# A fused decoder layer: queries and attention output in PSUM banks of their own, the scores of key tile 1 in the bank of tile 3

## What is computed

```
x = x + layernorm(attention(layernorm(x)))
x = x + layernorm(moe(layernorm(x)))

attention: q = rope(x @ Wq.T)                    16 heads of 128
           kp, vp = x @ Wkv.T                     one key and one value row per position
           k[h] = rope(kp * kh[h]); v[h] = vp * vh[h]     kh, vh: gated running sums
           p = softmax(causal(q k / sqrt(128)))
           o = p v;  return o @ Wout.T
moe:       8 experts of width 176, the best 2 per position, capacity 640 rows each,
           and a shared expert of width 704
```

## Time and profile before

| what | value |
|---|---|
| runs shown | 798.91, 798.91, 800.09 us; median 798.91 |
| profiled execution | 800.48 us, of which the span of the profile is 798.5 us |
| busy share of the span | PE 93%, PEld 78%, DVE 72%, ACT 59%, POOL 68% |
| chain that ended last, by engine | PE 73%, DVE 11%, issue 7%, ACT 4%, POOL 2%, DMA 2% |
| chain that ended last, most costly lines | L432 21%, L968 16%, L933 13%, L984 9%, L954 7%, all PE |
| L968, all in the loop | 512 matmuls, 149.5 us busy, mean 434 ns |
| L1340, all in the loop | 64 products, 44.3 us busy, mean 692 ns |

### The profile page before, as it was taken

How to read it: one execution, slowest core, us unless ns; L and a number is a source line. 1 busy time by engine, 2 the same in 40 slices (tenths; PEclk the granted TensorE clock), 3 DMA queues, 4 the chain that set the end, 5 groups by cost and what they waited for, 6 DMA issues and landing times.

```text
span 798.5 us, 14037 instructions
## 1 busy us (share of the span) xinstructions
PE 745.3 (93%) x4364; PEld 625.8 (78%) x4364; DVE 574.3 (72%) x1536; ACT 467.6 (59%) x1163; POOL 543.1 (68%) x459
## 2 busy tenths in 40 slices
PE   5799999999999999999999999998999989899992
PEld 4577788888888888887777888777778878898761
DVE  6967886768777767778887777898572357775685
ACT  5557776766676767666567666565623255653432
POOL 4457998787878887778888988778533534433663
PEclk9999999999999999999999999999999999999997
DMA  9411346422122222221222222221151134532332
GB/s 299 126 46 53 91 159 184 147 68 68 67 67 68 67 68 67 68 64 57 69 74 73 87 73 56 65 74 48 54 159 41 64 142 174 183 144 86 110 98 90
DMA packets 47748, 75.73 MB, mean 95 GB/s; under 512 B 9728, under 2 KB 24640, under 8 KB 47680
## 3 DMA queue, kind: packets, MB, share of 16 engines
q1 hardware_dynamic: 43504, 65.19, 25.9%
q0 software_dynamic: 3072, 8.39, 3.3%
q10 hardware_dynamic: 1104, 1.31, 0.5%
HBM read 57.71 MB, written 17.17 MB: 94 GB/s over the span
## 4 chain that ended last, share of the span: by engine, by line
PE 73%; DVE 11%; issue 7%; ACT 4%; POOL 2%; DMA 2%; DVEq 0%; ACTq 0%; POOLq 0%
PE ps L432 21%; PE ps L968 16%; PE ps L933 13%; PE ps L984 9%; PE ps L954 7%; PE ps L1130 5%; DVE q_sw L1312 1%; DVE q_sw L1311 1%; DVE hid_both L1643 1%; POOL slot_inputs L1784 1%; DVE hid_hi L1633 1%; POOL o_lo L1768 1%; DVE hid L1638 1%; DVE hid L1630 1%; DMA kvh_rows<-hc_t 1%
## 5 line engine op out<-in xcount | busy, mean ns | idle before, releaser
L968 PE MATMUL ps<-pt,vp 128*128 128x512 f32 (+3 forms) x512 | 149.5, 434 | 10.3 <-DVE q_sw L1312 10.1
L633 ACT ACTIVATE prob<-ps,neg_max 128x512 f32<-128x512 f32 (+3 forms) x256 | 132.5, 525 | 33.4 <-DVE neg_max L1321 30.6
L968 PEld LDWEIGHTS ps<-pt,vp 128*128 128x128 f32 x512 | 82.7, 190 | 59.9 <-issue 30.5
L1749 POOL TENSOR_TENSOR q_sw<-q_cos,q_sw 128x512 f32<-128x512 f32 x62 | 79.2, 1277 | 65.9 <-DVE q_cos L1313 65.8
L1321 DVE CUSTOM_DVE_ANT_0 ps<-ps,causal_row 128x512 f32<-128x512 f32 (+3 forms) x256 | 120.2, 511 | 4.6 <-PE ps L933 4.5
L642 ACT ACTIVATE pt<-ps,vcol 128x512 f32<-128x512 f32 x64 | 44.2, 690 | 109.4 <-PE ps L954 109.4
L1768 POOL TENSOR_TENSOR o_lo<-o_t,o_hi 128x512 fp32r<-128x512 f32 x64 | 84.4, 1318 | 33.4 <-ACT o_hi L671 33.4
L954 PE MATMUL ps<-id_f,prob 128*128 128x128 f32 x640 | 92.3, 275 | 0.9 <-ACT pt L642 0.9
L933 PE MATMUL ps<-k_hi,q_hi 128*128 128x512 f32 x248 | 86.6, 349 | 0.4 <-POOL q_lo L1753 0.3
L1340 DVE TENSOR_TENSOR o_t<-ps,inv_row 128x512 f32<-128x512 f32 x64 | 44.3, 692 | 52.5 <-PE ps L968 52.5
L1753 POOL TENSOR_TENSOR q_lo<-q_sw,q_hi 128x512 fp32r<-128x512 f32 x62 | 80.2, 1294 | 2.6 <-ACT q_hi L665 2.3
(11 more groups left out here) (218 smaller groups left out, 1942.3 us busy)
## 6 DMA issues: line engine op xcount, KB each, us to landing
kh_row<-kvh_rows SPq DMA_DIRECT2D x64, 256.0 KB, 3.2
inv_row<-inverse_sums SPq DMA_DIRECT2D x64, 256.0 KB, 3.1
slot_inputs<-zeros SPq DMA_DIRECT2D x8, 640.0 KB, 4.9
xg<-slot_inputs SPq DMA_DIRECT2D x8, 640.0 KB, 4.5
slot_outputs<-yo SPq DMA_DIRECT2D x8, 640.0 KB, 3.3
up_raw<-in_w_up_dram SPq DMA_DIRECT2D x8, 368.0 KB, 4.5
wo_raw<-in_wout_dram SPq DMA_DIRECT2D x4, 512.0 KB, 7.9
dn_sb<-in_w_dn_dram SPq DMA_DIRECT2D x8, 256.0 KB, 3.5
```

The lines of the kernel that those rows point to most:

```text
L633: ins = act.activation(prob[:, i % 2, ROW_AT[nt]:ROW_AT[nt] + w], ps_s[bank][:, at:at + w], ACT.Exp, scale=-1.0, bias=neg_max[:, i % 2, nt ...
L968: ins = pe.matmul(ps_qo[:, mt * P:SEQ], vp[:, b * TPB + mt, :], pt[:, i % 2, cols], start=(mt == 0), stop=(mt == PT_BANKS[-1][-1]))
L1749: pool.tensor_tensor(q_sw[:], q_cos[:], q_sw[:], ALU.add).then_inc(q_sum_ready, 1)
```

## The change

- Bank 0 holds queries alone (`ps_q`), bank 3 the attention output alone (`ps_o`). For units from 2 on the scores of tile 1 go to columns 0 to 255 of bank 1, behind those of tile 3: they wait until the exponentials of tile 3 of the same unit have read it, and the scores of tile 3 of a unit wait for all the exponentials of the unit before.
- `queries` waits for the rope products of the unit before only, `weigh_values` no longer for rope products.
- The routing pieces keep columns 256 and up of bank 3, now beside the output: `weigh_values(i)` waits until the former piece is out (`bank_free`, formerly `spare_free`), a piece waits for the divide of its step. `route_piece(i)` moves to the end of the step.
- The third group of scores moves behind `weigh_values`; the maxima and the exponentials of it move behind the divide and behind the output head.
- On VectorE `inverses(i + 1)` moves behind the layer norm and routing work of its step.

The diff without the renamed uses of the buffers and indices:

```diff
 PT_BANKS = [[0], [1, 3], [2]]
 
 
-def s_slot(nt):
-
-    return {3: (0, 0), 2: (1, 0), 0: (1, 384), 1: (2, 0)}[nt]
+def s_slot(i, nt):
+
+    return {3: (0, 0), 2: (1, 0), 0: (1, 384), 1: (0, 0) if i >= 2 else (2, 0)}[nt]
 
 
 def pt_slot(mt):
...
             return ctx.enter_context(nc.semaphore(name))
 
         ps = [ctx.enter_context(nc.psum_tensor(f"ps{i}", [P, 512], F32)) for i in range(8)]
-        ps_qo = ps[0]
+        ps_q = ps[0]
+        ps_o = ps[3]
         ps_s = [ps[1], ps[2], ps[3]]
         ps_pt = [ps[4], ps[5]]
         ps_acc = [ps[6], ps[7]]
...
                 if i == FACTOR_STEP:
                     factors_as_columns(1)
                 if i + 2 < UNITS:
-                    exps(i + 2, [1, 2])
+                    exps(i + 2, [1])
                 if i == UNITS - 2:
                     x_normed(ROUTED)
                 head_of_output(i)
+                if i + 2 < UNITS:
+                    exps(i + 2, [2])
                 for b, n in routes(i):
                     if 0 <= n < 4:
                         head_of_quarter(b, n)
...
                 if i:
                     pe.wait_ge(q_sin_ready, i)
                     pe.wait_ge(q_cos_ready, i)
-                if i >= 4:
-                    pe.wait_ge(o_ready, i - 3)
                 if i < H:
                     pe.wait_ge(wq_ready, wq_part(i) + 1)
                 h, b = head(i), batch(i)
-                three_pass(pe, ps_qo[:], lambda o: wq_hi[:, h, o, :], lambda o: wq_lo[:, h, o, :],
+                three_pass(pe, ps_q[:], lambda o: wq_hi[:, h, o, :], lambda o: wq_lo[:, h, o, :],
                            lambda o: xt_hi[:, o, tok(b)], lambda o: xt_lo[:, o, tok(b)]).then_inc(q_psum, 1)
 
             def scores(i, groups=range(3)):
...
                 r = i % 2
                 for k in groups:
                     tiles = S_BANKS[k]
-                    if i:
+                    if i >= 2 and k == 2:
+                        pe.wait_ge(exp_ready, 3 * i + 1)
+                    elif i >= 3 and k == 0:
+                        pe.wait_ge(exp_ready, 3 * i)
+                    elif i:
                         pe.wait_ge(exp_ready, 3 * (i - 1) + (k + 1))
                     for nt in tiles:
-                        bank, at = s_slot(nt)
+                        bank, at = s_slot(i, nt)
                         w = P * (nt + 1)
                         qs = slice(nt * P, (nt + 1) * P)
                         passes = ((q_rot, kh),) if i < PLAIN else ((q_hi, k_hi), (q_hi, k_lo), (q_lo, k_hi))
...
                     ins.then_inc(pt_psum, 1)
 
             def weigh_values(i):
-                n = min(i + 4, UNITS)
-                pe.wait_ge(q_sin_ready, n)
-                pe.wait_ge(q_cos_ready, n)
                 if i:
                     pe.wait_ge(o_ready, i)
+                else:
+                    pe.wait_ge(exp_ready, 6)
+                bank_free(i)
                 b = batch(i)
                 for k, tiles in enumerate(PT_BANKS):
                     pe.wait_ge((pt_first_ready, pt_second_ready, pt_rest_ready)[k], i + 1)
                     for mt in tiles:
                         cols = slice(COL_AT[mt], COL_AT[mt] + SEQ - mt * P)
-                        ins = pe.matmul(ps_qo[:, mt * P:SEQ], vp[:, b * TPB + mt, :], pt[:, i % 2, cols],
+                        ins = pe.matmul(ps_o[:, mt * P:SEQ], vp[:, b * TPB + mt, :], pt[:, i % 2, cols],
                                         start=(mt == 0), stop=(mt == PT_BANKS[-1][-1]))
                 ins.then_inc(o_psum, 1)
 
...
                         pe.wait_ge(pos_taken, b + 1)
 
             def route_piece(i):
-                spare_free(i)
                 for b, n in routes(i):
-                    if 0 <= n < 10 and i + 2 < UNITS:
-                        pe.wait_ge(exp_ready, 3 * (i + 2))
+                    if 0 <= n < 10:
+                        pe.wait_ge(o_ready, i + 1)
                     if 0 <= n < 4:
                         turn_quarter(b, n)
                     elif 4 <= n < 6:
...
                 if i + 2 < UNITS:
                     scores(i + 2, [0, 1])
                 turn_probs(i, [2])
-                route_piece(i)
-                if i + 2 < UNITS:
-                    scores(i + 2, [2])
                 if i == UNITS - 1:
                     turn(ROUTED)
                 weigh_values(i)
+                if i + 2 < UNITS:
+                    scores(i + 2, [2])
                 if i == FACTOR_STEP:
                     turn_factors(1)
                 if i == 1:
...
                     gather_output(i - 1)
                 if i + 4 < UNITS:
                     queries(i + 4)
+                route_piece(i)
             gather_output(UNITS - 1)
 
             def shared_up(j, tiles=range(SH)):
...
                     scaled_gates(1)
                 if i == 5:
                     sums_of_gates(1)
-                if i + 1 < UNITS:
-                    inverses(i + 1)
                 for b in range(B - 1):
                     n = i - back_step(b)
                     if n == 0:
...
                         choose(b)
                     elif n == POSITIONS + 1:
                         find_slots(b)
+                if i + 1 < UNITS:
+                    inverses(i + 1)
                 if i > 1 and wo_head(i - 2) is not None:
                     rest_of_wo(wo_head(i - 2))
                 if i + 3 < UNITS:
...
                     maxima(i + 2, [0])
                 rest_turned(i)
                 if i + 2 < UNITS:
-                    maxima(i + 2, [1, 2])
+                    maxima(i + 2, [1])
                 if i == UNITS - 1:
                     rest_of_turned(ROUTED)
                 divide_output(i)
+                if i + 2 < UNITS:
+                    maxima(i + 2, [2])
                 if i == 0:
                     dve.wait_ge(kt_ready, B)
                 if i == UNITS - 3:
```

## The result

The changed kernel takes 813.96 us (median of 6 runs, 812.52 to 816.39), the kernel before beside it 800.1 us (6 runs, 798.91 to 800.97): a ratio of 1.018, with an interval of 1.0159 to 1.0201. It is slower by 13.9 us where 7.7 were predicted, and 0.5 us above the range's top. The profiled execution is the slowest of the six, 816.39 us with a span of 814.4. That is 15.9 us over the span before. Among the six the span falls to 810.5 us as the mean granted clock of TensorE rises from 0.979 to 0.987 (0.989 in the profile before).

What follows compares the result with a forecast made beforehand. The prediction took TensorE alone to bound a plain step, with VectorE's lateness deciding its stalls. Terms -0.1 + 3.8 + 2.4 + 1.6 - 0.6 + 0.6 = +7.7 on 798.91 gave 806.6 us, range 798.0 to 813.5.

Steps and rivals of the forecast that it cites:

- The loss of 0.48 a quarter: Steps with a quarter routing piece: VectorE's rope products delayed 1.25 us, losing 0.48 each; eight steps, +3.8 us.
- 1.20 for the best experts: Two best-experts steps, waiting for turned logits: delay 1.97 us, loss 1.20 each, +2.4 us in all.
- 0.77 us as the time to spare: How late VectorE may be after the change before `weigh_values` loses time waiting for `rest_turned`; 0.48 us before.
- variances and shifts: Four stalls at 4-column VectorE operations held by GpSimd's run: `inverses` now uncovered, 0.44 - 0.29 each, +0.6 us.
- The start: First steps: queries stop waiting for the divide, tile-1 scores wait for late tile-3 exponentials (+2.5); together -0.1 us.
- step 3's stall: A stall of 1.36 us, predicted to be swallowed by the +2.5 us wait for exponentials in step 2.
- the 1.22 of the sum: First step: queries of unit 4 no longer wait for the divide, -0.98 - 0.24 = -1.22 us.
- The choice: Two steps choosing experts: same work, looser wait, -0.3 us each, -0.6 us in all.
- Slots: Two steps waiting for positions: delay 3.07 us, loss 2.30 against 1.49 before, +1.6 us in all.
- A: Rival, faster: the rope-product wait simply goes in nine late steps; 785.4 us at best, some 793 with pieces; chance 0.13.
- B: Rival, no change: routing pieces are absorbed with 1.25 us to spare instead of 0.77; 798.1 us; chance 0.11.
- C: Rival, much slower: no delay absorbed because the tile-1 chain binds the next step too; 812 to 819.7 us; chance 0.11.

Runs made afterwards that it cites:

- the run with the transposes: Changed kernel plus 19 unused identity transposes on TensorE in step 2, during its wait for the tile-3 exponentials: 813.0 us, ratio 1.0155.
- the repaired one: Changed kernel with `inverses` first on VectorE, routing pieces ahead of the queries, sigmoids later in step 2 and scatter DMAs moved: 794.8 us, ratio 0.9936.
- split changed kernel: The repaired one with `choose` and `find_slots` each cut into two halves in two steps: 801.83 us, ratio 1.0023.
- the run with the waits kept: Changed kernel with the two waits of `weigh_values` for the rope products of unit i + 3 kept: 830.74 us, ratio 1.0392.

## Why the prediction was half right

**The mechanism held.** `weigh_values` waits for `rest_turned`, the former wait for the divide at 64.35 is gone, TensorE waits for the tile-3 exponentials near 80 us, the chain holds `inverses` behind the routing work, and quarter steps take 8.7 us where "about 8.6" stood. The loss of 0.48 a quarter measured 0.53 to 0.61, that of 1.20 for the best experts 1.01 and 1.09. So 0.77 us as the time to spare was right within 0.2.

**The term that failed most: variances and shifts, +0.6, measured +5.0.** The step was "0.44 - 0.29, four times", from "`inverses` ran before it, covered; now behind, uncovered". Two things are missing. The blocked operation lasts until GpSimd's run ends, and that run ends later in the step. By the timelines of both kernels the run itself is 7.74 us long in both (394.10 to 401.84, and 400.86 to 408.60), and the operation lasts 4.61 us for 3.46 only because VectorE comes to it earlier. But the run ends 2.94 us behind the first transposes of the step (405.66) instead of 2.23 (399.61), and `inverses` stands behind it. With `inverses` back ahead these steps still take 9.91 and 9.73 us, 0.34 above before. There VectorE waits 1.04 us ahead of `inverses` in the step before, for tile 1's exponentials, which the change moved back (0.18 us in the kernel before); that this is the 0.34 was not tried apart. Second, the stall grew from 1.37 us to 2.08 and 1.88, and TensorE's clock fell behind it. The prediction has no term for that. By the start-to-start times from the weighing's two matmuls to the queries (3.87 and 3.70 us, 2.59 in a quarter step), 1.3 and 1.1 us of the +5.0 are half clock, plus 0.2 in the queries of batch 1. In the run with the transposes, where a stall of the same 2.08 us left the clock at 1.00, step 41 and the step behind take 10.43 + 7.98 us instead of 11.09 + 8.75, so 1.4 less. The rest of the +5.0, some 2.4, is the longer delay.

**The start, -0.1, measured +2.1.** The waits came as costed: 2.38 us of idle time for "+2.5", and step 3's stall was swallowed. The wait at the first queries is gone too; from the first scores to the first gather TensorE takes 10.86 us instead of 11.91, so 1.05 for the 1.22 of the sum. What was not in the sum is the half clock behind it, 1.5 us by the run with the transposes. The longest idle time of TensorE in the loop of before was 1.37 us, and the text took a wait of 2.5 us for no more than 2.5 us.

**The choice, -0.6, measured +1.2.** It was called "same work, looser wait". But the step ahead is late. With the best experts the rope products start 2.09 us behind the first transposes (363.24 against 361.15) instead of 0.25 (357.32 against 357.07), and GpSimd's products, which follow them, now run beside VectorE's next work: a layer norm operation (at 368.09) and the first of the choice, of 4 columns, take 1.26 and 1.25 us instead of 0.37 and 0.16, while a later one of 32 columns, 1.20 us before, takes 0.23. With pieces ahead of the queries 0.3 to 0.4 us of a choice step goes, with `inverses` ahead 0.13 to 0.15.

**Slots, +1.6, measured +0.5.** The sign was right, the size a third. GpSimd is idle from 388.84 and the two operations took 0.54 us, so the rope products came 2.74 us late (at 390.68, with the step's first transposes at 387.90, less the usual 0.04) and not the 3.07 assumed. The loss is 1.76 us a step (9.85 less 7.96 and the 0.13 of the positions), 0.27 above the 1.49 of before, where the sum had 2.30. The Trainium skill, GPSIMD Engine Reference, section Key points, says that GpSimd and VectorE instructions with two SBUF inputs contend. The trace agrees: the two operations take 1.40 us beside a busy GpSimd, 0.54 where it stops on the way, and 0.29 beside an idle one (the third batch, at 593.11 in the kernel before).

**The rivals.** A fell: the wait did not simply go. B fell: quarter steps were not 8.2 us. C named the total (812 to 819.7) but not the cause, for tile 1's chain ends nothing last in the loop beyond step 2. The half clock is in no case of the prediction. In the profiled execution it is 1.5 + 1.3 + 1.3 = 4.1 us; with it taken off, the +15.3 would be +11.2 against +7.7.

The Trainium skill, Perfetto Trace Analysis, section Matmuls, has independent groups rotate through banks, so that the emptying of one overlaps the next group. The trace agrees where the bank is what is waited for (16.8 us in the new order). Private banks give nothing that can be told where the next wait in the queue stands close behind (794.8 against 793.32 us): at choice and slots the kernel before with moved scatters waits 0.87 and 1.25 us for rope products, the repaired one 0.83 and 0.83 us for `rest_turned`.

## What to carry to other kernels

Ahead of taking a resource conflict away, list what stands behind it in the waiting engine's queue: the next wait in the same queue may be 0.29 us away, and the order that comes with the new freedom may cost more than it gives (813.96 against 800.1 us here). When work moves on one engine, look at what then waits for it on the others: with the scores moved on TensorE alone, the divide stood behind a maximum that came later. Move work on an in-order engine only after having looked at what covered it: `inverses` cost nothing ahead of the routing work, and 8.9 us behind it. Where a stall of TensorE grows, cost the work behind it too, which may run at half the granted clock; and where a 4-column operation takes microseconds, look at the neighbour that holds it, for moving that one's work was the cheapest gain here (0.9%).

## What the hardware showed beyond expectation

**TensorE's clock.** In the loop, idle times of 1.71 us and less left the granted clock at 1.00 in every run. It fell to 0.50, for 3 to 4 us, behind idle times of 1.76 (split changed kernel, at 514.63), 1.88 (changed, at 554.81), 2.08 (changed, at 412.26), 2.23, 2.38 and 2.50 us, and the long weighings behind 2.18 and 2.49 us (3.82 and 3.84 us) say the same. But the length of the idle time does not decide alone: it stayed at 1.00 behind 1.88 us in the run with the waits kept (436.66), behind 1.96 us in the kernel before with scores moved (372.97), behind 2.08 us at the same place in the run with the transposes, and behind 2.11 us in the split changed kernel (396.92). Between executions of one kernel the number of such stretches may differ; the six runs of the changed kernel, 810.5 to 814.4 us with a mean clock of 0.987 to 0.979, fit that, though only one of them was profiled. What decides is left open.

**VectorE behind GpSimd.** The 4-column operation waited for more than one instruction of GpSimd: four of 1.23 to 1.30 us, one right behind the other from 403.56 to 408.60, passed before it ended. The Trainium skill, SBUF — State Buffer, section Who interferes with whom, says that of a VectorE instruction in a two-port mode and a GpSimd instruction, whichever comes first holds the shared ports for its whole length and the other is blocked. The trace agrees with the block, though no run shows in which mode this operation is. It adds that a block can outlast one instruction. It need not: in the step of the choice (VectorE and GpSimd of the changed kernel) two operations end about as one GpSimd product ends, though the next product follows at once:

```profile
368.09 1.26 DVE L1385 TENSOR_SCALAR y_back<-y_back,mv,rstd 128x256 f32<-128x256 f32 x1
369.15 1.34 POOL L1773 TENSOR_TENSOR o_lo<-o_t,o_hi 128x512 fp32r<-128x512 f32 x1
369.27 1.25 DVE L1444 TENSOR_TENSOR gap<-top 128x4 f32<-128x4 f32 x1
370.46 1.29 POOL L1768 TENSOR_TENSOR kh_row<-kt,kh_row 128x512 f32<-128x512 f32 x1
```

What decides between the two is left open.
